# A six-stage decoder kernel: keys scaled by ScalarE, two stage borders reordered, idle products taken out

## What is computed

```
x = x + L0_attn(ln(x))    # latent attention: 32 heads, key and value latent of 4
x = x + L0_xattn(ln(x), ctx, ctx, mask)   # q = x, k = v = ctx, 32 heads on 8 key heads
x = x + L0_ffn(ln(x))     # x W_up^T + LoRA (rank 8) of the expert with the top logit
x = x + L1_attn(ln(x))    # six powers of a gate, fused, + silu FFN of width 1248
x = x + L1_xattn(ln(x), ctx)              # energy over the channel axis, skip product
x = x + L1_ffn(ln(x))     # relu^2 FFN of 1024 + latent expert path, layernorm
```

```
scores = einsum('bsgrd,btgd->bgrst', xq, xk) / sqrt(16) + mask
probs = softmax(scores)
out = einsum('bgrst,btgd->bsgrd', probs, xv)
```

## Time and profile before

| | us |
|---|---|
| median of 3 runs | 1218.9 |
| lowest and highest of them | 1215.52, 1219.99 |
| the profiled execution, its own time | 1212.91 |
| its span in the trace | 1211.2 |
| PE busy | 1114.7 (92%) |
| DVE, ACT, POOL busy | 691.5, 473.4, 420.9 |

### The profile page before, as it was taken

The page is one execution under the profiler, slowest core; times in us unless marked ns, Lnnn a source line. Parts: engine busy times, 40 slices in busy tenths (PEclk is TensorE's granted clock), DMA queues, the critical chain, the costliest instruction groups (busy, mean ns, idle before and its releaser), DMA issues.

```text
span 1211.2 us, 23648 instructions
## 1 busy us (share of the span) xinstructions
PE 1114.7 (92%) x9380; PEld 597.2 (49%) x9380; DVE 691.5 (57%) x1221; ACT 473.4 (39%) x829; POOL 420.9 (35%) x369
## 2 busy tenths in 40 slices
PE   7878996998998889999999999999989889999996
PEld 3444553776675444444444444444556544444442
DVE  6777674687787674535312521522289933656465
ACT  4566672675654553322111211211257622322231
POOL 2245475888882230000280060000043400325163
PEclk8887886899999999999999999999999989999998
DMA  7000000111120220310010000000000000000001
GB/s 238 2 2 4 22 10 14 41 43 36 38 77 4 64 64 22 101 52 34 19 61 20 1 20 32 0 1 1 0 12 9 2 1 1 12 24 17 17 27 44
DMA packets 29011, 35.91 MB, mean 30 GB/s; under 512 B 5882, under 2 KB 20499, under 8 KB 28788
## 3 DMA queue, kind: packets, MB, share of 16 engines
q1 hardware_dynamic: 27506, 34.53, 8.9%
q10 hardware_dynamic: 1410, 0.06, 0.1%
HBM read 30.24 MB, written 4.19 MB: 28 GB/s over the span
## 4 chain that ended last, share of the span: by engine, by line
PE 64%; DVE 12%; issue 3%; ACT 3%; POOL 0%; DVEq 0%; POOLq 0%; ACTq 0%
PE p_up L116 10%; PE p_up L117 10%; PE p_up L118 10%; PE p_y L116 8%; PE p_y L118 8%; PE p_y L117 8%; PE p_y L1527 3%; DVE e_den L2234 2%; PE p_up L1492 1%; PE p_up L1515 1%; DVE wd_lo L103 1%; PE p_up L110 1%; DVE st L188 1%; PE p_up L1497 1%; PE p_y L110 1%
## 5 line engine op out<-in xcount | busy, mean ns | idle before, releaser
L1926 DVE TENSOR_TENSOR d_h_low<-d_hf,d_h_high 128x512 f16<-128x512 f32 (+1 forms) x40 | 27.8, 695 | 205.1 <-ACT d_h_high L2015 205.1
L116 PE MATMUL p_up<-d_xt_high,wd_hi 128*128 128x512 f16 (+1 forms) x352 | 133.4, 379 | 2.9 <-PE p_y L118 1.5
L117 PE MATMUL p_up<-d_xt_low,wd_hi 128*128 128x512 f16 (+1 forms) x352 | 133.4, 379 | 0.0
L118 PE MATMUL p_up<-d_xt_high,wd_lo 128*128 128x512 f16 (+1 forms) x352 | 133.4, 379 | 0.0
L170 ACT ACTIVATE d_sg<-p_up 128x512 f32<-128x512 f32 (+1 forms) x40 | 23.7, 594 | 212.8 <-PE p_up L118 212.8
L116 PE MATMUL p_y<-wd_hi,d_h_high 128*128 128x512 f16 (+1 forms) x272 | 103.1, 379 | 0.0
L118 PE MATMUL p_y<-wd_hi,d_h_low 128*128 128x512 f16 (+1 forms) x272 | 103.1, 379 | 0.0
L117 PE MATMUL p_y<-wd_lo,d_h_high 128*128 128x512 f16 (+1 forms) x272 | 103.1, 379 | 0.0
L138 POOL TENSOR_SCALAR wd_raw<-wd_raw 128x1156 f32<-128x1156 f32 x8 | 25.1, 3137 | 207.1 <-DVE d_h_low L1926 207.1
L435 POOL TENSOR_TENSOR a_pt_low<-a_ex,a_pt_high 128x1024 f16<-128x1024 f32 x32 | 68.0, 2126 | 80.3 <-ACT a_pt_high L924 80.2
L2196 POOL TENSOR_TENSOR wd_hi<-wd_hi,e_den 128x1024 f32<-128x1024 f32 x16 | 30.5, 1907 | 147.3 <-DVE e_den L2236 147.3
(11 more groups left out here) (340 smaller groups left out, 2938.9 us busy)
## 6 DMA issues: line engine op xcount, KB each, us to landing
wd_raw<-in_w_d SPq DMA_DIRECT2D x16, 616.0 KB, 3.7
wd_raw<-in_w_f SPq DMA_DIRECT2D x8, 578.0 KB, 3.8
X<-in_x SPq DMA_DIRECT2D x4, 1024.0 KB, 12.3
wd_lo<-in_ctx_t SPq DMA_DIRECT2D x128, 32.0 KB
out_x<-wd_raw SPq DMA_DIRECT2D x16, 256.0 KB, 2.0
wd_lo<-in_ctx SPq DMA_DIRECT2D x32, 64.0 KB, 2.4
wd_raw<-in_w_c SPq DMA_DIRECT2D x1, 1096.0 KB, 12.4
wd_hi<-in_Wo SPq DMA_DIRECT2D x1, 1024.0 KB
```

Of the source, the lines that this page charges most:

```text
L116: nc.tensor.matmul(ps, st[0], mv[0], start=start, stop=False)
L117: nc.tensor.matmul(ps, st[0], mv[1], start=False, stop=False)
L118: return nc.tensor.matmul(ps, st[1], mv[0], start=False, stop=stop)
L1926: nc.vector.tensor_tensor(hid[1][0:n, d % NH, :], value, hid[0][0:n, d % NH, :], ALU.subtract).then_inc(h_ready, 1)
```

## The change

1. Stage a: `light` is gone, and with it the 40 idle products of the steps.
2. Stage b: the scaling of the keys moves from GpSimd to ScalarE (`keys(t, h)`), one call each unit at the end of ScalarE's round. `keys(t, h)` waits until GpSimd has read `ks` (`bd_ready`), and GpSimd waits for `ks_ready`. `fetch` now waits for the two ScalarE readers of `kt`.
3. Border of b and c: VectorE does `norm_o` ahead of `low_p` in the last two units; `p.c.norm` comes two units earlier on ScalarE, `p.c.trans` two units earlier on TensorE, `p.c.low` on VectorE in unit 30, `p.c.high` (the start of stage c before) on ScalarE in unit 30, and tile 0's products of stage c (`p.c.aux`, `p.c.main`) stand ahead of `attend(30)`.
4. Stage c: each weight instruction of ScalarE is cut into two halves, one ahead of `high_z`, one after `norm`. `products` is cut into `aux` and `main`, and `aux(t)` goes ahead of `delta(t - 1)`.
5. Border of e and f: the norms of tiles 2 and 3 of stage f go ahead of the last `total`, and `turn_one(2)`, `turn_one(3)` ahead of `e.output(14)`.

```diff
@@ stage_a
-        def light(c, j):
-            weight = sum({"T": 0.85, "L": 3.2, "Q": 0.3, "O": 0.64, "P": 0.64}.get(use[0], 0) for use in chunk_uses(c, j))
-            return max(0, math.ceil((0.5 - weight) / 0.16))
...
-                        keep_warm(light(n // 8, n % 8))
@@ part_b, sync
-                    sp.wait_ge(bd_ready, 2 * t + 1)
+                    sp.wait_ge(bd_high, 2 * t - 2)
+                    sp.wait_ge(ks_ready, 2 * t - 2)
@@ part_b, gpsimd
-                    if fresh:
-                        wait_apart(pool, kt_in[b], 128 * (TC // 2 * c + i // 2), held.apart)
...
-                        nc.gpsimd.tensor_scalar(ks, kt[:, b, :, :].rearrange("p k n -> p (k n)"),
-                                                held.mask_bs[:, h:h + 1], None, ALU.mult).then_inc(ks_ready, 1)
@@ part_b, vector
-                    if n == N + 1:
+                    if n >= N - 2:
+                        norm_o(n - 2)
+                    if 0 <= n < N:
+                        low_p(n)
+                    if 2 <= n < N - 2:
+                        norm_o(n - 2)
+                    if n >= 2 and n % 2:
+                        add(n // 2 - 1)
+                    if n == N - 2:
                         p.c.low(v, 0)
                         p.c.low(v, 1)
...
@@ part_b, scalar
+                def keys(t, h):
+                    act.wait_ge(bd_ready, 2 * t + 3 + h)
+                    nc.scalar.activation(ks, kt[:, t % 2, :, :].rearrange("p k n -> p (k n)"), ACT.Copy,
+                                         scale=held.mask_bs[:, h:h + 1]).then_inc(ks_ready, 1)
...
-                    if n in (N - 4, N - 2):
-                        p.c.norm(act, (n - N + 4) // 2)
+                    if n in (N - 6, N - 4):
+                        p.c.norm(act, (n - N + 6) // 2)
...
+                    if n == N - 2:
+                        p.c.high(act, 0)
+                        p.c.high(act, 1)
...
+                    if n % 2 and n // 2 + 3 < NT:
+                        keys(n // 2 + 3, 0)
+                    if n % 2 == 0 and n // 2 + 2 < NT:
+                        keys(n // 2 + 2, 1)
@@ part_b, tensor
-                    if n == N:
+                    if n == N - 2:
                         p.c.trans(pe, 0)
                         p.c.trans(pe, 1)
+                    if n == N - 1:
+                        p.c.aux(pe, 0)
+                        p.c.main(pe, 0)
@@ part_c, scalar
+            piece(t, 0)
             high_z(act, t)
             if t + 2 < NT:
                 norm(act, t + 2)
-            if t in EARLY:
-                weights[0](EARLY.index(t))
-            if t - 1 in EARLY:
-                weights[1](EARLY.index(t - 1))
+            piece(t, 1)
@@ part_c, tensor
-        products(pe, 0)
         for t in range(1, NT):
             turn_z(pe, t - 1)
...
+            aux(pe, t)
             delta(pe, t - 1)
-            products(pe, t)
+            main(pe, t)
@@ part_e, vector
         update(v, NT - 3)
+        norm_next(2)
+        norm_next(3)
         total(v, NT - 1)
@@ part_f, vector and tensor
-                norm_first(v, 2)
-                norm_first(v, 3)
...
-                e.output(pe, NT - 2)
                 turn_one(2)
                 turn_one(3)
+                e.output(pe, NT - 2)
```

More of the change, by code:

```diff
@@ L1457, in scalar @@
                 high_keys(1)
+                keys(1, 0)
                 high_keys(2)
                 for n in range(-2, N):
-                    if n in (N - 4, N - 2):
-                        p.c.norm(act, (n - N + 4) // 2)
+                    if n in (N - 6, N - 4):
+                        p.c.norm(act, (n - N + 6) // 2)
                     if n >= 0:
@@ L1706, in scalar, with piece @@
     def scalar(act, weights, high_next):
-        high(act, 0)
-        high(act, 1)
+        def piece(t, half):
+            if t in EARLY:
+                weights[0](EARLY.index(t), half)
+            if t - 1 in EARLY:
+                weights[1](EARLY.index(t - 1), half)
         nc.scalar.activation(ident_h[:], held.ident[:], ACT.Copy).then_inc(ident_ready, 1)
@@ L1735, in trans, with aux @@
         transpose_tile(nc, held, p_t(t), xn[:, t % 2, :]).then_inc(t_ready, 1)
-    def products(pe, t):
+    def aux(pe, t):
         st = [x[:, t % 2, :, :] for x in xt]
@@ L1744, in products, with main @@
         last.then_inc(aux_ready, 1)
+    def main(pe, t):
+        st = [x[:, t % 2, :, :] for x in xt]
         if t >= 2:
@@ L1778, in tensor @@
         turn_next(3)
-    p.low, p.norm, p.trans = low, norm, trans
+    p.low, p.norm, p.trans, p.high, p.aux, p.main = low, norm, trans, high, aux, main
     p.gpsimd, p.vector, p.scalar, p.tensor = gpsimd, vector, scalar, tensor
@@ L1841, in low_first, with high_first, scale_first @@
                                         ALU.subtract).then_inc(wd_split, 1)
-            def high_first(act, q):
-                part = slice(PD * q, PD * q + PD)
+            def high_first(act, q, half):
+                part = slice(PD // 2 * half, PD // 2 * half + PD // 2)
+                into = slice(PD * q + part.start, PD * q + part.stop)
                 act.wait_ge(wd_in[q % 2], 16 * (q // 2) + 16)
-                nc.scalar.activation(held.wd_hi[:, part], raw[:, q % 2, :], ACT.Copy, scale=WS).then_inc(wd_high, 1)
-            def scale_first(act, q):
-                act.wait_ge(wd_high, q + 1)
-                nc.scalar.activation(raw[:, q % 2, :], raw[:, q % 2, :], ACT.Copy, scale=WS).then_inc(wd_scaled, 1)
+                nc.scalar.activation(held.wd_hi[:, into], raw[:, q % 2, part], ACT.Copy, scale=WS).then_inc(wd_high, 1)
+            def scale_first(act, q, half):
+                part = slice(PD // 2 * half, PD // 2 * half + PD // 2)
+                act.wait_ge(wd_high, 2 * q + 1 + half)
+                last = nc.scalar.activation(raw[:, q % 2, part], raw[:, q % 2, part], ACT.Copy, scale=WS)
+                if half:
+                    last.then_inc(wd_scaled, 1)
             def gpsimd(pool):
```

12 lines of the change are left out of this document (3 added, 9 removed).

## The result

The median went from 1219.45 us (4 runs) to 1197.28 us (4 runs, 1196.90 to 1201.21): ratio 0.983, 95% interval 0.980 to 0.986. The forecast was 1196.5 us. The total was met, in part by luck: the traces show that two terms of the sum (stages a and b) were not, and the difference between median and trace that the sum carried over was gone.

A forecast was written before the change was run, and what follows sets the result against it. TensorE was taken as busy but underclocked in stages a and b, with GpSimd bounding stage b from 284 us on. Gains 12.4 + 2.0 + 0.5 + 5.5 + 2.0 = 22.4 us took the median 1218.9 to 1196.5, range 1187 to 1209.

The forecast's parts named there:

- the difference between median and trace that the sum carried over: Whole kernel: timed median 1218.9 us against profiled 1212.9, 6.0 us more, carried over unchanged into the forecast.
- the 9 at which the forecast was to fail: Stage b: the forecast fails if its gain is under 9 us, being more than half of the sum.
- a sign against it: Stage a: a clock of 0.50 between 160 and 185 us would show the forecast wrong.
- Stage b, 12.4 us: Units 2 to 28: keys on ScalarE relieve GpSimd, TensorE runs without a stop; gain 12.4 us, ends 9 and 13.
- Stage a, 2 us: Idle products out: 3.7 us gained at unchanged clock, less clock losses; 2 us gain, ends 4.5 gain and 4 loss.
- The price of the clock: Stage a: half clock costs about 1.3 us a step, 4 to 5 us if it hits steps 24 to 27.
- Rival A: Clock falls in stage a: loss of 4 us, perhaps 2 more in the first chunk; about 1203 us, chance 0.27.
- Border of b and c, 0.5 us: Reordered work starts stage c's first `update` earlier; gain 0.5 us, ends 2.3 gain and 1 loss.
- 1.8 us against 2.3: Border of b and c: 2.3 us gained by reordering, 1.8 lost to half clock after TensorE's wait.
- Stage c, 5.5 us: Halved weight instructions shorten ScalarE's round, 12 tiles x 0.46; gain 5.5 us, ends 3.5 and 6.5.
- Border of e and f, 2 us: Two norms moved to where GpSimd is idle, 1.0 us instead of 2.7; gain 2.0 us, ends 0 and 2.3.
- Rivals B and C: Stage b. B: ScalarE becomes the bound, 1206, chance 0.08. C: GpSimd and ScalarE block each other over `ks`, slower, 0.03.

The follow-up runs named there:

- experiment 2: The changed kernel with SyncE's loads at the end of stage b spread out instead of issued in one go: 1195.35 us, ratio 0.981 to the kernel before.
- experiment 9: The changed kernel with spread loads and all 40 idle products, plus 17 more where TensorE waits anyway (steps 4 and 12): 1197.08 us, ratio 0.983 to before.

## Why the prediction was right, and where not

The forecast said 1196.5 us and the median is 1197.28, with the range of 1187 to 1209 around it. By its own signs it was not a clean hit: stage b gained 4.9 us in the first trace, under the 9 at which the forecast was to fail, and 10.8 in the second; the clock was 0.50 from 336.9 to 350.6, and between 160 and 170, where that was to be a sign against it. Term by term:

- **Stage b, 12.4 us.** The step that ruled it holds: GpSimd was the bound, TensorE takes its place, and ScalarE's two instructions fit. The sum gives 121.0 us from unit 2 to unit 28; six of the eight traces with ScalarE's keys at their own price have 121.3. The changed kernel itself has 128.6 and 123.7. The step that failed is the one on SyncE: I looked at the queue of `fetch` and not at what stands behind it, a burst that reaches TensorE through its code (experiment 2). The same burst was in the trace of before, without such a stop, and I had no row on it. It cost 7.3 us in one trace and 2.4 in the other. A smaller slip: that each stop behind GpSimd was followed by a lower clock. Behind the first one, which ended at 286.7, the clock stayed at 1.00 until 299.6.
- **Stage a, 2 us.** The sign was wrong or the effect nil. The part on the path was right (1.0 us in steps 10 and 18). The price of the clock was set at 1.3 us a step for steps 24 to 27, where it is small: steps 24 to 26 took 3.6, 3.6 and 4.4 us, mostly at half clock, in after and 3.3, 3.2 and 4.0 before, since ScalarE is the path there. It was missed in steps 2 to 8. Rival A, with its "2 us more in the first chunk", had the place, and its clock of 0.50 came, but not its size: it asked for 6 to 8 us above the forecast, and taken out alone the products cost 2.2 us by the medians, some 4 above it. Without the products the granted clock from 0 to 202 us was 0.71 to 0.78, with them 0.83 to 0.87. The Trainium skill (TensorE: Matmul & The Clock Gate, section Why this matters for your kernels) says that activity holds the higher level; the traces agree with its direction. A higher clock was not a shorter time here, though, and more products (experiment 9) gained nothing.
- **Border of b and c, 0.5 us.** From unit 28 to the first update 2.4 us went against the usual 28 us; the profiled execution of before, 26.3, was a lucky one. I had set 1.8 us against 2.3 for the half clock behind it, and about 1 us of it is in the first interval of stage c, which is as long with the idle products out alone. Alone the part gave 0.1 us by the medians. The size holds better than its parts.
- **Stage c, 5.5 us.** 6.05 over the twelve rounds (0.50 each, since a half takes 0.60 until the next starts and not 0.65), less the first interval: 4.7 and 5.6 in the two traces. The alternation of 3.95 and 4.7 us came out as worked out from GpSimd and the gate.
- **Border of e and f, 2 us.** 2.2 in both traces.
- **Not forecast:** 1.2 to 1.3 us in stage e and about 0.6 us in stage f. In stage e it is one interval between two `total`, 6.6 or 6.7 us instead of 5.4, with `turn` (L2369) at half clock from 886 to 888. It is in six traces, all of kernels with the second to fifth part of the change together. The two others of that kind (loads spread, with no or with some products) have as long a stretch of half clock in stage e, but some 6.5 us earlier in it, where it costs nothing; so have two kernels without these parts together (idle products out alone, the border of b and c alone). So the place of the half clock decides; what sets it is open. Stage f is not of the change: it took 236.8 to 238.0 us over all traces, and 237.9 in the last two, where it is as before.

So the median was met for reasons that I had only in part, and by luck for the rest. Alone, the parts give by the medians 14.7 us (keys), 7.2 (stage c), 0.1 (border of b and c) and -2.2 (idle products out); with the 2.2 of the border of e and f, which only traces show, that is 22.0. The forecast had 12.4, 5.5, 0.5, 2.0 and 2.0: too little for keys and stage c, too much for stage a, and each of these medians can be off by 3 to 4 us. Trace against trace the gain is 11.7 and 12.6 us, not 22.4; the forecast for a profile like the one shown, 1190.5, was missed by 10.7 us. The rest lies between the traces and the medians: both traced executions of before (1212.91, 1210.68) are among its fastest, 6.5 and 5.3 us under the medians of their sets, while the changed kernel's traces (1201.21, 1198.11) lie 3.9 us above and 1.0 under theirs. I had carried the 6.0 us over unchanged, and in the changed kernel they are gone. What they are in before, no trace of it shows. Its stops behind GpSimd, with stretches of low clock behind most of them, are one candidate, since keys alone gained 14.7 us by the medians and 12.7 from unit 2 to unit 28; that is an argument, not a measurement. The half clock at the start of stages c and d is another: neither trace of before has it behind the first `update`, but those of stage c alone, of the idle products out alone and of the border of b and c alone do, and the two together cost 3.0 to 3.8 us in each.

Rivals B and C did not come: ScalarE idles in every unit and GpSimd ends 2 us ahead. Putting all products back and spreading the loads gives the lowest median here, 1192.15 us. By the ratio to before, 0.981 (0.978 to 0.985), it can't be told from the spread loads alone (0.981) or the products alone (0.979); the changed kernel's 0.983 and 0.984 are 2 to 6 us above the three, with intervals that overlap.

## What to carry to other kernels

Where an engine needs 1 us a tile more than TensorE, and TensorE starts with a lead, the gain of relieving it is read from TensorE's own undisturbed pace over all tiles: the measured stretch less that pace. Moving a job to an engine was safe here as long as its rounds still showed idle time; all its waits in a tile counted as room, not only the one ahead of the next critical step. Read the queue of loads to its end: a burst for a later stage stopped TensorE in the middle of work that waits for nothing, by holding up its next instructions, and stop and half clock together cost four to six times the stop. A change that adds or takes out a few instructions moves the code against such a burst, and can win or lose by that alone. Idle products should be judged by the time of the steps behind them, over several traces and many runs: here they raised the clock in every trace and did not shorten the kernel clear of the noise, since one execution of the same stage varies by more than they are worth.

## What the hardware showed that was not expected

- TensorE stopped for 1.29 and 0.60 us inside a run of products, ahead of the same product in both traces, at the end of 4 us with the DMA engines at 0.93 and 0.89. The packet of its code had started 3.0 and 2.6 us later than without the burst. It ran at 1.2 GHz for some 13 and 3 us afterwards.
- The same code of stage a took 137.1 to 145.5 us in eight traces with the products, 140.0 to 151.1 in four without: the place where the clock falls differs between executions by some us, and steps 2 to 8 are where it shows most.
- A ScalarE instruction of 128x64 between SBUF tiles costs 0.25 us in a row of eight (2.0 for 8) where one of 128x512 costs 0.72: cutting an instruction into eight costs 2.8 times as much.
- VectorE's L103 takes 0.49 us for 128x512 with GpSimd idle and 1.34 with it busy (2.68 for two), and the 128x4 of L1638 0.22 and 0.97.
